# Spreading the even rows of a token-dependent feed-forward over the partitions: products with a picking matrix, or a store and a load through DRAM

## The reference, cut to what matters

```python
lt = x[:, 1:17, :]                       # 16 tokens of each batch
even = lt[:, ::2, :]                     # tokens 1, 3, ..., 15 of the batch
odd = lt[:, 1::2, :]                     # tokens 2, 4, ..., 16
m1 = (even[:, :4, :, None] * odd[:, :4, None, :]).reshape(B, 1024, 256)
m2 = (even[:, 4:, :, None] * odd[:, 4:, None, :]).reshape(B, 256, 1024)
h = gelu(einsum('bsd,hd->bsh', x, W1) + scale * einsum('bsd,bhd->bsh', x, m1) + b1)
out = einsum('bsh,oh->bso', h, W2) + scale * einsum('bsh,boh->bso', h, m2) + b2
```

## Time and profile before

| | us |
|---|---|
| median of 3 runs (2439.45 to 2443.52) | 2440.02 |
| the profiled execution, its own time | 2429.65 |
| its span | 2428.0 |
| of it stage 3 | about 332 |

### The profile page before, as it was taken

One profiled execution on the slowest core, in us unless ns is written; L12 is line 12 of the kernel. 1 busy time (PEld: TensorE's weight loads), 2 busy tenths in 40 slices (PEclk: granted clock), 3 DMA queues, 4 the chain that ended last, 5 costly groups with the idle time before them and its releaser, 6 DMA issues. The chain is left out here.

```text
span 2428.0 us, 47281 instructions
## 1 busy us (share of the span) xinstructions
PE 1854.6 (76%) x13556; PEld 1372.1 (57%) x13557; DVE 1609.0 (66%) x3925; ACT 989.6 (41%) x2052; POOL 1125.3 (46%) x1472
## 2 busy tenths in 40 slices
PE   5878888888888888888499997856235169999862
PEld 3436676666666666767366765433125148887431
DVE  8947777777778777877755452587764964444454
ACT  3436666666666666655123232323022013333100
POOL 4125555555555555553121210376750035555576
PEclk9979999999999999999799998878566569999986
DMA  4679999999999999999312100000001344548444
GB/s 154 217 242 342 335 342 339 325 349 319 353 322 356 323 352 315 353 337 290 105 49 70 59 11 3 0 0 1 0 5 65 146 137 154 155 150 144 118 131 124
DMA packets 296148, 460.84 MB, mean 190 GB/s; under 512 B 38316, under 2 KB 229532, under 8 KB 295964
## 3 DMA queue, kind: packets, MB, share of 16 engines
q1 hardware_dynamic: 267484, 392.06, 49.4%
q0 software_dynamic: 28480, 66.39, 10.4%
HBM read 236.91 MB, written 221.38 MB: 189 GB/s over the span
## 5 line engine op out<-in xcount | busy, mean ns | idle before, releaser
L987 DVE CUSTOM_DVE_ANT_0 c2p<-bank,c2p 128x512 f32<-128x512 f32 x512 | 350.7, 685 | 204.8 <-PE bank L883 178.5
L945 ACT ACTIVATE c2p<-c2p,neg_max 128x512 f32<-128x512 f32 x512 | 371.9, 727 | 14.0 <-DVE neg_max L987 14.0
L996 DVE COPY probsT<-bank 128x512 f32<-128x512 f32 x512 | 351.2, 686 | 32.0 <-PE bank L893 31.2
L960 ACT COPY a_stage<-bank 128x320 f32<-128x320 f32 (+1 forms) x512 | 210.3, 411 | 346.3 <-PE bank L852 206.0
L893 PE MATMUL bank<-ident,c2p 128*128 128x128 f32 x2048 | 316.1, 278 | 1.0 <-ACT c2p L945 0.9
L893 PEld LDWEIGHTS bank<-ident,c2p 128*128 128x128 f32 x2048 | 254.8, 144 | 8.7 <-issue 2.0
L2261 POOL DMA_INDIRECT p_x_tile<-y_d,p_token x160 | 152.5, 953 | 228.5 <-POOLq L1962 107.4
L883 PE MATMUL bank<-ident,p2c 128*128 128x128 f32 x1280 | 231.9, 280 | 0.0
L852 PE MATMUL bank<-tab,q 96*128 96x320 bf16 (+1 forms) x512 | 157.3, 307 | 78.4 <-ACT a_stage L960 78.3
L864 PE MATMUL bank<-tab,k 96*128 96x320 bf16 (+1 forms) x512 | 158.1, 309 | 46.7 <-DVE b_stage L939 27.1
L878 PE MATMUL bank<-k,q 96*128 96x384 bf16 (+1 forms) x512 | 158.0, 309 | 34.9 <-issue 27.8
(11 more groups left out here) (295 smaller groups left out, 3868.5 us busy)
## 6 DMA issues: line engine op xcount, KB each, us to landing
p2c_d<-b_stage SPq DMA_DIRECT2D x64, 640.0 KB, 7.9
c2p_d<-a_stage SPq DMA_DIRECT2D x64, 640.0 KB, 6.2
p2c_d<-b_stage SPq DMA_DIRECT2D x64, 576.0 KB, 8.4
c2p_d<-a_stage SPq DMA_DIRECT2D x64, 576.0 KB, 7.1
p2c<-p2c_d SPq DMA_DIRECT2D x256, 144.0 KB, 5.3
c2p<-c2p_d SPq DMA_DIRECT2D x256, 144.0 KB, 5.3
o_sorted_d<-p_o_pair SPq DMA_DIRECT2D x80, 256.0 KB, 2.3
p_w_all<-in_experts SPq DMA_DIRECT2D x4, 3072.0 KB, 21.9
```

The costliest lines, as they stand in the source:

```text
L945: act.activation(c2p[:, w % 4, j, :], c2p[:, w % 4, j, :], ACT.Exp, bias=neg_max[:, w % 2, j:j + 1], scale=-1.0).then_inc(exp_done, 1)
L960: act.copy(staged(a_stage, wa % 2, wa % TPB)[:, j, :], bank[A_BANK][:, 0:width(wa % TPB)]).then_inc(a_copied, 1)
L987: dve.tensor_tensor_reduce(c2p[:, w % 4, j, :], bank[S_BANKS[(HB * w + j) % 3]][:], c2p[:, w % 4, j, :], -SCALE, LOWEST, ALU.add, ALU.min, ...
L996: dve.tensor_copy(probsT[:, wp % 2, j], bank[T_BANKS[j % 2]][:].rearrange("p (k q) -> p k q", k=TPB)).then_inc(probsT_copied, 1)
```

## The change

The picking matrix, its setting, the eight products and their semaphores go. After y's first tile of a batch is there, SP stores its eight even rows (8 KB) to DRAM, waits for the store to land, and loads the 8 KB back to each of 128 partitions (1 MB) into a new tile `even`, from which VectorE makes the weights. On SP these steps for batch b - 2 stand ahead of the loads of batch b, and for the last two batches behind the loop, ahead of the weight loads of stage 4.

```diff
+        even_d = dram("even_d", [2, 2 * LOW, C], F32)
...
-        pick = sb(early3, "p3_pick", [P, 2 * LOW, P], side="right")
...
-                    pool.memset(pick[:], 0.0).then_inc(pick_set, 1)
-                    pool.wait_ge(pick_set, 1)
-                    pool.affine_select(out=pick[:], in_=pick[:], compare_op=ALU.not_equal, fill=1.0, base=-1,
-                                       pattern=[[-2, 2 * LOW], [0, P]], channel_multiplier=1).then_inc(pick_set, 1)
...
+            even = sb(st, "p3_even", [P, 2 * LOW, C])
+            even_stored, even_loaded = [[sem(f"p3_even_{k}{u}") for u in range(2)] for k in ("stored", "loaded")]
...
+                    def even_rows(b, u):
+                        use = 16 * (b // 2 + 1) if isinstance(b, int) else 8 * (b - u) + 16
+                        sp.wait_ge(lnB["normed"], TPB * b + 1)
+                        apart(sp)
+                        sp.dma_start(even_d[u], y[1:4 * LOW:2, 0, :]).then_inc(even_stored[u], 16)
+                        sp.wait_ge(even_stored[u], use)
+                        sp.dma_start(even[:].rearrange("p i c -> p (i c)"),
+                                     even_d[u:u + 1].rearrange("o i c -> o (i c)").broadcast_to([P, 2 * LOW * C])
+                                     ).then_inc(even_loaded[u], 16)
+
+                    def body(b, u):
+                        if not isinstance(b, int) or b >= 2:
+                            even_rows(b - 2, u)
+                        load(b, u)
...
-                    batches(sp, load)
+                    batches(sp, body)
+                    for u in range(2):
+                        even_rows(B - 2 + u, u)
...
                         if not isinstance(b, int) or b > 1:
-                            pe.wait_ge(w_ready, W_OPS * (b - 1) + W1_OPS)
+                            pe.wait_ge(o_ready, 2 * b)
...
                         pe.wait_ge(lnB["normed"], TPB * b + TPB)
+                        wait_count(pe, yT_ready, CC * b)
...
-                        pe.wait_ge(yT_ready, CC * b + CC)
-                        pe.wait_ge(o_ready, 2 * b + 2)
-                        for i in range(2 * LOW):
-                            last = pe.matmul(bank[EVEN_BANKS[i // 2]][:, (i % 2) * C:(i % 2 + 1) * C], pick[:, i, :],
-                                             y[:, 0, :], start=True, stop=True)
-                        last.then_inc(even_made, 1)
...
-                        wait_count(dve, even_made, b)
+                        wait_count(dve, yT_made, CC * b)
...
-                        dve.wait_ge(even_made, b + 1)
+                        dve.wait_ge(even_loaded[u], 16 * (b // 2 + 1) if isinstance(b, int) else 8 * (b - u) + 16)
...
-                                    w1_b[:, u, c, i * C:(i + 1) * C], even(i), odd[:, c, i:i + 1],
+                                    w1_b[:, u, c, i * C:(i + 1) * C], even[:, i, :], odd[:, c, i:i + 1],
...
-                                    w2_b[:, u, c:HID:CC, cols], even(LOW + i).rearrange("p (n q) -> p q n", q=LOW),
+                                    w2_b[:, u, c:HID:CC, cols], even[:, LOW + i, :].rearrange("p (n q) -> p q n", q=LOW),
```

More of the change, by code:

```diff
@@ L111, in build @@
         ctx_d = dram("ctx_d", [H, B, 2 * D, S], F32)
+        HID = FFN // P
+        LOW = 4
         rsum_d = dram("rsum_d", [H, B, S], F32)
+        even_d = dram("even_d", [2, 2 * LOW, C], F32)
         def batches(eng, body):
@@ L188, in row @@
             return a[name].rearrange("(o n) -> o n", o=1).broadcast_to([P, a[name].shape[0]])
-        HID = FFN // P
-        LOW = 4
         early3 = ExitStack()
-        pick = sb(early3, "p3_pick", [P, 2 * LOW, P], side="right")
         attn = ExitStack()
@@ L259, in build @@
             v_stored, v_ones_set = sem("p1_v_stored"), sem("p1_v_ones_set")
-            pick_set = sem("p1_pick_set")
             Y_BANKS, M_BANKS, V_BANK, FAR_BANK = (0, 1), (2, 3, 4, 5), 6, 7
@@ L1043, in build @@
                 "wo_made", "n_bo_ready", "x_lb_ready", "o_ready", "scaled", "x1_ready", "x1_b2_ready")]
-            yT_made, yT_ready, even_made, odd_ready, w1_ready, w_ready = [sem("p3_" + k) for k in (
-                "yT_made", "yT_ready", "even_made", "odd_ready", "w1_ready", "w_ready")]
+            yT_made, yT_ready, odd_ready, w1_ready, w_ready = [sem("p3_" + k) for k in (
+                "yT_made", "yT_ready", "odd_ready", "w1_ready", "w_ready")]
             ffn1_made, gelu_done, ffn2_made, x2_ready = [sem("p3_" + k) for k in (
@@ L1048, in build @@
             O_BANKS, Y_BANKS, F_BANKS, G_BANKS = (0, 1), (2, 3), (4, 5, 6, 7), (6, 7)
-            EVEN_BANKS = O_BANKS + Y_BANKS
             W1_OPS = CC * LOW
@@ L1269, in weights @@
                         dve.wait_ge(odd_ready, b + 1)
-                        dve.wait_ge(even_made, b + 1)
+                        dve.wait_ge(even_loaded[u], 16 * (b // 2 + 1) if isinstance(b, int) else 8 * (b - u) + 16)
                         wait_count(dve, ffn2_made, 2 * (b - 1))
-                        def even(i):
-                            return bank[EVEN_BANKS[i // 2]][:, (i % 2) * C:(i % 2 + 1) * C]
                         for c in range(CC):
```

## The result

| | before | after |
|---|---|---|
| median of 11 runs, us | 2440.02 | 2417.93 |
| lowest to highest | 2430.62 to 2450.37 | 2411.47 to 2434.74 |
| profiled execution, its own time | 2429.65 | 2426.84 |
| stage 3 in it, first projection to the end of the last residual add | 329.8 | 309.5 |

The ratio after to before is 0.9912, 95% interval 0.9891 to 0.9934: faster by 22 us where 19 were forecast, well above the 0.2% that can be told.

What follows compares the result with a forecast made beforehand. TensorE was taken to bound stage 3, picking products included. A late start of 11.3 us less 30.1 from seven transitions gives -18.8, so 2440.0 becomes 2421 us; range 2413 to 2437.

Steps and rivals of the forecast that it cites:

- Products on the path: TensorE in stage 3: without picking products each of seven transitions saves 4.3 us, 30.1 in all; period 37.89 to 33.6.
- the clock dip in before's profile: In one batch the picks took 5.41 us instead of 3.72 at granted clock 0.50; this 1.7 us was left out.
- Gelu and the residual adds hide: Stage 3: last Gelu ends 1.06 us before the transposes do; residual adds end T0 + 29.7, second products T0 + 30.3.
- Round trip: Rows through DRAM per batch: store to next issue 2.38 us, load to landing L = 6.5, ends 4.4 and 11.1.
- the w2T row: Trace's 1 MB w2T load with others around it, 5.9 us; starting point for the new load's time to landing.
- the bias window: Bias broadcast at stage start, 229 GB/s against 373 plain; a third of the resulting 1.8 us was added to the load.
- Threshold: Load time to landing L decides the period from 7.5 us, then costs one for one in six transitions.
- the second loop: From POOL's n_bo through o-adds, norms, y, store, load and weights back to n_bo: 32.6 us against 33.6, 1.0 to spare.
- the rival of a load at 8 to 9 us: Load just misses its cover: -12.2 us at 8.3, -7.3 at 9; chance 0.18 for loads of 7.5 to 9.5.
- My sign for a wrong forecast: VectorE waiting for a DMA at its weights and, behind it, an o-add waiting for POOL rather than TensorE.
- The start: Batch 0 of stage 3 has no cover: first products start 11.3 us late, waiting for weights behind store and load.
- Weights from SBUF: 16 VectorE instructions a batch: 485 ns from SBUF against 477 from PSUM, 1 us in all, off the path.

Runs made afterwards that it cites:

- the products kept: Changed kernel with eight products of the picks' shape put back behind the transposes, result unread: stage 3 341.8 us, period 37.9 to 38.0, one run 2453.2 us.
- the different rows: Changed kernel with the 1 MB load reading 128 different rows of an input array: load lands in 5.0 us against 4.7, stage 3 307.3 us.
- the load twice: Changed kernel with the 1 MB load of the even rows repeated after the first landed: stage 3 322.7 us, periods 33.5 to 37.3.
- the store twice: Changed kernel with the 8 KB store repeated after the first landed: stage 3 311.9 us, period 33.45 to 33.53.

## Why the prediction was right

*Products on the path: right.* Forecast 4.3 us a transition, period 33.6; measured 4.4 and 33.5, and put back by the products kept. The six transitions from batch 1 on took 225.8 us and take 197.4, 28.4 less where 25.8 were forecast; 1.7 of that is the clock dip in before's profile, which I had left out. The seventh, out of batch 0, was counted at the same 4.3 and gave 2.1: its o-add came 1.5 us later behind the slower second weights, and the gap ahead of its transposes was 2.3 us instead of 1.4.

*Gelu and the residual adds hide: right.* No wait on either shows behind the transposes.

*Round trip: sized too dear.* Store and wait 1.79 instead of 2.38; load 4.7 instead of 6.5; against them the second weights 4.8 instead of 3.2. The 0.6 us that I put on reading one row 128 times was wrong, as the different rows show; the other 1.2 came from starting at the w2T row, a load with others around it. Why the bias window had a lower rate no run shows; small and ending transfers are my guess.

*Threshold: wrong by its own term.* I took the norms in the second loop at the length they had while TensorE set the pace, 14.2 us with the o-adds. Two waits for ScalarE inside shrink when VectorE is late: 12.2. So the load decides not from L = 7.5 but, with this and the other terms, from about 4.7 + 3.8 = 8.5, an estimate from the run with the load twice. By it the rival of a load at 8 to 9 us would have cost less than I wrote, and a load would have had to take about 11 us to eat the whole gain: (20.3 + 4.7 + 6 x 8.5) / 7 = 10.9. My sign for a wrong forecast, an o-add that waits for POOL, was no sign either: with the store twice it showed at an unchanged period.

*The start: right in place, near in size.* 11.3 forecast, 10.0 measured. It is made of other parts: the row sums' store took 3.43 us and not 2.38, the round trip 6.6 and not 8.9.

*Weights from SBUF.* For the first weights the row held (479 ns for 477). For the second I read a row without the step, and it didn't hold: 673. It cost 1.3 us at the start and nothing later. The Trainium skill, "SBUF — State Buffer", section "Door 1: The DMA port swizzle", says that an access crossing to a new line of 16 bytes pays a penalty and that full rate needs at least two accesses a line. A step of 16 bytes makes one access a line, and the three measurements (480 in line, 673 and 665 with a step) agree; its further statement that a step of 4 float32 is free does not.

*Sum.* Stage 3: 10.26 late at the first products, 2.13 regained in batch 0, 28.41 in the six transitions: -20.28. Forecast -18.8, median -22.1. The mechanism is the forecast one, but that the sum came so near is in part luck: the start was 1.0 us cheaper, the six transitions gave 2.6 more, and batch 0 gave 2.2 less. The step of 1.8 us from the stage to the medians lies inside their scatter.

## What to carry to other kernels

When an engine's line is full, a cheap instruction on it costs its whole length, and a slow detour through DRAM costs nothing if its loop is shorter. Sum that second loop with its inner waits at their least, not only as they stand in the trace, and look for the one pass that has no cover: the first, where the order of one queue cost 10 us beside a gain of 20. Before moving an operand from PSUM to SBUF, look at its step.

## What the runs showed of the hardware

- A two-operand VectorE instruction of 128x256 float32 takes 476 ns with the stepped operand (16 bytes) in PSUM, 480 with all in SBUF in line, 673 with that step in SBUF, 665 with a large step on the other two operands.
- One 8 KB row loaded to 128 partitions (1 MB) lands in 4.7 us, 128 different rows of 8 KB in 5.0.
- A store of 8 KB and the wait for it take 1.8 us to the next issue; a store of 256 KB took 2.38 in one profile and 3.43 in another.
- With the load issued twice, one of its landings took 6.5 us where the median is about 4.5. Its cause stays open.
